# Pairwise bilinear interaction with a three-layer top network: first layer in two steps of two output tiles, its seventh input tile as two 64-row matmuls

## The reference, cut to what matters

```python
e = jnp.stack([tbl_f[ids[:, f]] for f in range(40)], axis=1)     # 2048 x 40 x 64
i_idx, j_idx = np.triu_indices(40, k=1)                          # 780 pairs
z = einsum('bpe,bpe->bp', einsum('bpd,pde->bpe', e[:, i_idx], W), e[:, j_idx])
h = jnp.concatenate([z, dense_ctx], axis=1)                      # 2048 x 796
h = jnp.maximum(h @ W_top1 + b_top1, 0.0)                        # 796 -> 512
h = jnp.maximum(h @ W_top2 + b_top2, 0.0)                        # 512 -> 256
y = h @ W_top3                                                   # 256 -> 1
```

## Time and profile before

| what | value |
|---|---|
| median of three runs | 1220.74 us |
| profiled execution: span on the core | 1221.2 us |
| PE busy | 1123.9 us (92%) |
| DVE busy | 957.6 us (78%) |
| ACT busy | 928.2 us (76%) |
| POOL busy | 633.7 us (52%) |
| mean share of the 16 DMA engines, by slice | 1 to 4 tenths |
| granted clock of PE, slices behind the first four | 0.9 or more of full speed |
| first layer L755: records, busy | 224 of mean 598 ns, 99.6 us |

### The profile page before, as it was taken

How to read it: one execution, slowest core, us unless ns; L and a number is a source line. 1 busy time by engine, 2 the same in 40 slices (tenths; PEclk the granted TensorE clock), 3 DMA queues, 4 the chain that set the end, 5 groups by cost and what they waited for, 6 DMA issues and landing times.

```text
span 1221.2 us, 45331 instructions
## 1 busy us (share of the span) xinstructions
PE 1123.9 (92%) x17376; PEld 401.1 (33%) x17376; DVE 957.6 (78%) x833; ACT 928.2 (76%) x6893; POOL 633.7 (52%) x742
## 2 busy tenths in 40 slices
PE   0468899999999999999999999999999999999999
PEld 0112333333333333333343333333333333333333
DVE  0258899999875688999967579999985768999970
ACT  0158878987676688999957588998967678998971
POOL 7877776555566555555556545544545554520000
PEclk9988999999999999999999999999999999999999
DMA  4122222222212222223222122222221212212100
GB/s 172 26 67 70 70 71 68 88 87 68 86 44 64 64 55 75 66 65 104 64 62 86 43 63 85 64 62 83 64 85 42 86 41 62 85 57 67 58 13 0
DMA packets 34199, 81.80 MB, mean 67 GB/s; under 512 B 12144, under 2 KB 12672, under 8 KB 33856
## 3 DMA queue, kind: packets, MB, share of 16 engines
q1 hardware_dynamic: 13472, 57.88, 14.3%
q0 software_dynamic: 20480, 21.01, 7.6%
q10 hardware_dynamic: 32, 0.01, 0.0%
HBM read 78.84 MB, written 0.01 MB: 65 GB/s over the span
## 4 chain that ended last, share of the span: by engine, by line
PE 53%; ACT 19%; DVE 11%; issue 11%; POOL 5%; DMA 0%; DVEq 0%; ACTq 0%
PE Ups L714 21%; ACT PB L555 17%; PE Zps L734 11%; PE Ups L707 9%; PE Ups L755 8%; DVE P L652 6%; DVE PB L641 3%; POOL VN L537 3%; DVE zB L625 2%; PE Ups L762 2%; PE Ups L693 2%; ACT P L574 1%; POOL stage L537 1%; ACT V L567 1%; POOL rest L534 1%
## 5 line engine op out<-in xcount | busy, mean ns | idle before, releaser
L555 ACT ACTIVATE PB<-PB 128x64 f32<-128x64 f32 x3344 | 801.1, 244 | 102.8 <-DVE PB L641 99.9
L652 DVE TENSOR_TENSOR P<-Ups,V 128x1024 f32<-128x1024 f32 x504 | 600.6, 1216 | 186.0 <-PE Ups L714 183.5
L537 POOL DMA_INDIRECT stage<-tbl,idx x512 | 483.2, 944 | 359.6 <-PE Ups L714 149.6
L555 ACT ACTIVATION_READ_ACCUMULATOR PB<-PB 128x1 f32 x3344 | 635.2, 190 | 0.0
L714 PE MATMUL Ups<-V,wf 64*32 64x512 f32 x8384 | 546.0, 600 | 32.4 <-ACT V L567 16.7
L641 DVE TENSOR_TENSOR PB<-Ups,VN 128x1024 f32<-128x1024 f32 x256 | 311.3, 1217 | 39.4 <-PE Ups L707 32.3
L707 PE MATMUL Ups<-wf,V 64*32 64x512 f32 x4096 | 279.2, 600 | 7.3 <-ACT V L567 2.8
L734 PE MATMUL Zps<-P,sel 64*32 64x512 f32 x4192 | 283.4, 591 | 0.0
L714 PEld LDWEIGHTS Ups<-V,wf 64*32 64x32 f32 x8384 | 149.5, 107 | 325.6 <-issue 168.0
L537 POOL DMA_INDIRECT VN<-tbl,idx x128 | 121.1, 946 | 93.1 <-PE Ups L714 39.0
L734 PEld LDWEIGHTS Zps<-P,sel 64*32 64x32 f32 x4192 | 81.6, 108 | 140.3 <-issue 134.2
(11 more groups left out here) (23 smaller groups left out, 110.1 us busy)
## 6 DMA issues: line engine op xcount, KB each, us to landing
wf<-w_units SPq DMA_DIRECT2D x84, 640.0 KB
stage<-tbl,idx POOLq DMA_INDIRECT x512
VN<-tbl,idx POOLq DMA_INDIRECT x128, 2.4
w1s<-w SPq DMA_DIRECT2D x1, 1792.0 KB, 11.0
w2s<-w SPq DMA_DIRECT2D x1, 512.0 KB, 11.9
idx<-ids SPq DMA_DIRECT2D x1, 320.0 KB, 3.0
z<-dense_t SPq DMA_DIRECT2D x4, 32.0 KB
y<-z ACTq DMA_DIRECT2D x4, 2.0 KB
```

The costliest lines, as they stand in the source:

```text
L537: pool.indirect_dma_start(out=natural_rows(m, t)[:, D * f:D * f + D], out_offset=None, in_=tables[field][:, :], in_offset=bass.IndirectOff ...
L555: last = act.activation(p, p, ACT.Copy, accum_out=zB[:, t, at:at + 1])
L652: dve.tensor_tensor(p, Ups[:, slot, :, :rows], v, ALU.mult).then_inc(mul_done, 1)
```

## The change

The first layer is done in two steps (`L1_STEPS`) of two output tiles each: a step fills both banks of its slot. It goes through tiles 1 to 6 of `z` with 128 x 128 weights for the first output tile and then for the second, and ends with two matmuls for tile 0, one for each bank, that use only 64 of the array's rows: the first reads rows 0 to 63 of tile 0, the second rows 64 to 127. For that, both halves of tile 0 hold all of its 32 rows. SP loads the dense inputs twice, and copies the strips of four rows from each half into the other by four small DMAs, all from its place ahead of one weight chunk. The weights of tile 0 are laid out by the host in the same doubled way. ACT does two activations behind each first-layer step. A group's top network has five steps instead of seven, 14 units apart instead of 10. The costs in `step_us` follow. The second and third layers are as before, under new numbers.

```diff
--- before.py
+++ after.py
@@ -176,7 +176,11 @@
 
 U_SLOTS, P_SLOTS, PB_SLOTS, STAGE_SLOTS = 3, 8, 3, 4
 LAG = 3
-MLP_STEPS = N1 // P128 + N2 // P128 + 1
+L1_STEPS, L2_STEPS = 2, N2 // P128
+MLP_STEPS = L1_STEPS + L2_STEPS + 1
+LAYER3 = MLP_STEPS - 1
+STRIP_ROWS = 2 * PART_ENDS[0]
+DENSE_LOADS = 2 * 3
 
 W_COLS, WB_COLS = 2 * D, 2 * JP * D
 CHUNK, W_SLOTS = 10 * W_COLS, 3
@@ -243,7 +247,7 @@
 
 
 RUN_PAIRS, TIES_US, RAMP_UNITS = 6, 62.0, 60
-MLP_APART = 10
+MLP_APART = 14
 
 
 def red_at(q):
@@ -301,7 +305,7 @@
 
 def step_us(step):
     if step[0] == "mlp":
-        return 6.15 if step[2] < 4 else 3.6 if step[2] < 6 else 0.7
+        return 11.1 if step[2] < L1_STEPS else 3.6 if step[2] < LAYER3 else 0.7
     return STEP_US[step[0]]
 
 
@@ -392,6 +396,11 @@
 Z0_BEFORE = {quad_units(_g * QUADS + PART_ENDS[0] - 1)[-1] + LAG + 1: _g for _g in range(GROUPS)}
 
 
+def outs_before(g, x):
+
+    return g * (4 + L2_STEPS + 1) + (2 * x if x < L1_STEPS else 4 + x - L1_STEPS)
+
+
 def z0_tile(g):
 
 
@@ -502,8 +511,14 @@
                 for g in range(GROUPS):
                     if c == w_of(J_LAST[g])[0] + 4:
                         sp.wait_ge(z0_done, g + 1)
-                        sp.dma_start(z[DENSE_ROW:DENSE_ROW + DENSE, z0_tile(g), :SIZES[g]],
-                                     dense_t[:, FIRST_ROW[g]:FIRST_ROW[g] + SIZES[g]]).then_inc(dense_loaded, 16)
+                        for half in range(2):
+                            at = D * half + DENSE_ROW
+                            sp.dma_start(z[at:at + DENSE, z0_tile(g), :SIZES[g]],
+                                         dense_t[:, FIRST_ROW[g]:FIRST_ROW[g] + SIZES[g]]).then_inc(dense_loaded, 16)
+                            for at in (0, 32):
+                                source, to = D * (1 - half) + at, D * half + at + STRIP_ROWS
+                                sp.dma_start(z[to:to + STRIP_ROWS, z0_tile(g), :],
+                                             z[source:source + STRIP_ROWS, z0_tile(g), :]).then_inc(dense_loaded, 16)
                 x = W_SETS[min(group, 1)] + load
                 sp.dma_start(wf[:, c % W_SLOTS, :], w_units[:, x * CHUNK:(x + 1) * CHUNK]
                              ).then_inc(wf_loaded[c % W_SLOTS], 16)
@@ -576,12 +591,12 @@
                 elif kind == "z0":
                     act.wait_ge(red_done, g * QUADS + PART_ENDS[0])
                     if g > 1:
-                        act.wait_ge(mlp_done, (g - 2) * MLP_STEPS + 4)
+                        act.wait_ge(mlp_done, (g - 2) * MLP_STEPS + L1_STEPS)
                     act.copy(z[:, z0_tile(g), :rows], Zps[:, 0, :rows]).then_inc(z0_copied, 1)
                 elif kind == "z":
                     act.wait_ge(red_done, g * QUADS + PART_ENDS[x])
                     if g:
-                        act.wait_ge(mlp_done, (g - 1) * MLP_STEPS + 4)
+                        act.wait_ge(mlp_done, (g - 1) * MLP_STEPS + L1_STEPS)
                     if g and 2 * x - 1 == H2:
                         act.wait_ge(y_written, 16 * g)
                     act.copy(z[:, 2 * x - 1:2 * x + 1, :rows], Zps[:, :, :rows]).then_inc(z_done, 1)
@@ -597,14 +612,17 @@
                     if g == 0 and x == 0:
                         act.wait_ge(consts_loaded, 16 * 5)
                     act.wait_ge(mlp_done, g * MLP_STEPS + x + 1)
-                    if x < 4:
-                        act.activation(h1[:, x, :rows], out, ACT.Relu, bias=b1s[:, x:x + 1]).then_inc(mlp_out, 1)
-                    elif x < 6:
-                        act.activation(z[:, H2 + x - 4, :rows], out, ACT.Relu, bias=b2s[:, x - 4:x - 3]
-                                       ).then_inc(mlp_out, 1)
+                    if x < L1_STEPS:
+                        for bank in range(2):
+                            n = 2 * x + bank
+                            act.activation(h1[:, n, :rows], Ups[:, slot, bank, :rows], ACT.Relu,
+                                           bias=b1s[:, n:n + 1]).then_inc(mlp_out, 1)
+                    elif x < LAYER3:
+                        n = x - L1_STEPS
+                        act.activation(z[:, H2 + n, :rows], out, ACT.Relu, bias=b2s[:, n:n + 1]).then_inc(mlp_out, 1)
                     else:
                         act.copy(z[:, H2, :P128], out[:, :P128]).then_inc(mlp_out, 1)
-                        act.wait_ge(mlp_out, (g + 1) * MLP_STEPS)
+                        act.wait_ge(mlp_out, outs_before(g + 1, 0))
                         act.dma_start(y[FIRST_ROW[g]:FIRST_ROW[g] + rows, :].rearrange("(t n) o -> t (n o)", n=P128),
                                       z[0:P128:32, H2, :P128]).then_inc(y_written, 16)
 
@@ -678,7 +696,7 @@
                 elif kind == "ztr":
                     pe.wait_ge(z_done, Z_COUNT[("zb", g, 0)])
                 else:
-                    pe.wait_ge(mlp_out, g * MLP_STEPS + x + 1)
+                    pe.wait_ge(mlp_out, outs_before(g, x + 1))
 
             for step in PE_STEPS:
                 kind, g, x = step
@@ -743,28 +761,35 @@
                             last = pe.transpose(Ups[:, slot, h, P128 * t:P128 * (t + 1)],
                                                 zB[:, t, P128 * h:P128 * (h + 1)], ident[:, :])
                     last.then_inc(ztr_done, 1)
-                elif x < 4:
+                elif x < L1_STEPS:
                     if x == 0:
                         pe.wait_ge(consts_loaded, 16 * 5)
-                        pe.wait_ge(dense_loaded, 16 * (g + 1))
-                    ready = [s for s in Z_STEPS if s[1] == g]
-                    tiles = [(None, z0_tile(g))] + [(s, k) for s in ready for k in z_tiles(s)]
-                    for n, (s, k) in enumerate(tiles):
-                        if x == 0 and s:
-                            pe.wait_ge(z_done, Z_COUNT[s])
-                        last = pe.matmul(Ups[:, slot, 0, :size], w1s[:, k % ZT, P128 * x:P128 * (x + 1)], z[:, k, :size],
-                                         start=n == 0, stop=n == ZT - 1)
+                    tiles = [(s, k) for s in Z_STEPS if s[1] == g for k in z_tiles(s)]
+                    for bank in range(2):
+                        n = 2 * x + bank
+                        for i, (s, k) in enumerate(tiles):
+                            if n == 0:
+                                pe.wait_ge(z_done, Z_COUNT[s])
+                            pe.matmul(Ups[:, slot, bank, :size], w1s[:, k, P128 * n:P128 * (n + 1)], z[:, k, :size],
+                                      start=i == 0, stop=False)
+                    if x == 0:
+                        pe.wait_ge(dense_loaded, 16 * DENSE_LOADS * (g + 1))
+                    for bank in range(2):
+                        n, half = 2 * x + bank, slice(D * bank, D * bank + D)
+                        last = pe.matmul(Ups[:, slot, bank, :size], w1s[half, 0, P128 * n:P128 * (n + 1)],
+                                         z[half, z0_tile(g), :size], start=False, stop=True)
                     last.then_inc(mlp_done, 1)
-                elif x < 6:
+                elif x < LAYER3:
+                    n = x - L1_STEPS
                     for k in range(4):
-                        if x == 4:
-                            pe.wait_ge(mlp_out, g * MLP_STEPS + k + 1)
-                        last = pe.matmul(Ups[:, slot, 0, :size], w2s[:, k, P128 * (x - 4):P128 * (x - 3)],
+                        if n == 0:
+                            pe.wait_ge(mlp_out, outs_before(g, 0) + k + 1)
+                        last = pe.matmul(Ups[:, slot, 0, :size], w2s[:, k, P128 * n:P128 * (n + 1)],
                                          h1[:, k, :size], start=k == 0, stop=k == 3)
                     last.then_inc(mlp_done, 1)
                 else:
                     for k in range(2):
-                        pe.wait_ge(mlp_out, g * MLP_STEPS + 5 + k)
+                        pe.wait_ge(mlp_out, outs_before(g, L1_STEPS + k + 1))
                         for t in range(TILES[g]):
                             last = pe.matmul(Ups[32 * t:32 * t + 1, slot, 0, :P128], w3s[:, k:k + 1],
                                              z[:, H2 + k, P128 * t:P128 * (t + 1)], start=k == 0, stop=k == 1)
@@ -796,14 +821,20 @@
     for n, item in enumerate(A_ITEMS):
         for block, half, i, j, _, _ in unit_pairs(item):
             row, tile = z_place(2 * n + block, half)
-            w1[row, tile] = W1[first[i] + j]
+            if tile:
+                w1[row, tile] = W1[first[i] + j]
+            else:
+                for to in range(2):
+                    away = row // D != to
+                    w1[D * to + row % D + STRIP_ROWS * away, tile] = W1[first[i] + j]
     for k in range(B_ROWS):
         for b in range(2):
             for j in range(2 * JP):
                 at = 4 * JP * (B_ROWS - 1 - k) + 2 * JP * b + j
                 w1[at % P128, ZB_TILE + at // P128] = W1[first[2 * k + b] + 2 * J0 + j]
     pairs = F * (F - 1) // 2
-    w1[DENSE_ROW:DENSE_ROW + DENSE, 0] = W1[pairs:]
```

(2 more changed lines are left out.)

## The result

The changed kernel takes 1230.72 us in the median (1227.71 to 1230.88), the kernel before 1220.74 us beside it: a ratio of 1.0076 with a 95% interval of 1.0061 to 1.0090, so it is slower, where 5.4 us less were forecast. The timed runs of the changed kernel are 1.8 us longer than their spans. Timed runs of the kernel before beside later experiments on equally fast chips have spans of 1217.5 to 1220.2 us, so its profiled execution, with 1221.2, was slower than all of them; the profiled one of after has 1229.0. That is why the two traces lie 7.8 us apart and the medians 10.0.

The account below looks back on a forecast made before the run. PE was taken to bound the kernel nearly everywhere; its own work -7.0, ACT behind steps +0.6 and the pauses' places +1.0 gave -5.4 us, so 1215.3 us in the median, with an 8-in-10 range of 1212.9 to 1219.8.

Parts of the forecast that it names:

- What bounds the kernel: Whole kernel: PE is the limit nearly everywhere behind the ramp, busy 1123.9 of 1221.2 us, DVE and ACT just behind.
- The first layer in the loop and the tail: PE's first-layer steps: 6.2 us gained in the loop's three groups and 0.8 in the tail, together -7.0 us.
- The change of block inside a step: PE, first-layer step: switching from 128 x 128 to 64 x 128 blocks costs 0.20 us, between 0.10 and 0.25.
- The way out: PE, end of a first-layer step in the loop: going to 64 x 32 blocks costs 0.05 us, between nothing and 0.10.
- The pair: PE, tile 0's two 64-row matmuls: halves run side by side and cost one matmul's 0.86 us; one behind the other, 1.72.
- the prediction's sign: What the trace should show for tile 0: 64-row records in pairs starting within 0.05 us, two pairs 0.43 us apart.
- SP: Six small DMAs instead of one hold a weight chunk up by 1.9 us; some 25 us cover it, so nothing is lost.
- ACT behind a step: Second activation delays ACT's next work by 0.59 us; loop steps cost nothing to 3.5 us, 0.6 taken.
- The place of the pauses: First-layer steps are pauses where ACT and DVE catch up; moving them costs nothing to 3.0 us, 1.0 taken.
- POOL: Five gathers go in a step of 11.1 us where three went in 6.15; counted nothing, give or take 1 us.
- slower: the long step starves the others: Rival: sums queued during long steps stall PE behind them, 1.7 us a step, 10 in all; about 1224.5 us, chance 0.08.
- ACT and DVE take most of it back: Rival: ACT and pause costs at their ends, 3.5 and 3.0 us, leave 0.5 us gain, 1220.2 us; chance 0.10.

Follow-up runs that it names:

- e3: Changed kernel without the sixteen small DMAs that copy strips of tile 0 between the halves; 1228.53 us, ratio 1.0069 to the kernel before.
- m1: Kernel before with its top-network steps 20 units apart instead of 10, on a slower chip; 1314.16 us, ratio 0.9941.
- f2: Kernel before with transposes and gathers where the planner puts them for the changed kernel, transposes kept behind steps; 1232.75 us, ratio 1.0080.
- g1: Changed kernel with one planner constant 1.6 instead of 1.9, so six gathers instead of five go ahead of a long step; 1224.85 us, ratio 1.0029.
- q2: Changed kernel with 12 of 16 sums of each of ACT's units left out; 1203.33 us, ratio 0.9855 to the kernel before.
- q1: Kernel before with 12 of 16 sums of each of ACT's units left out; 1208.12 us, ratio 0.9896.
- h0: Changed kernel whose planner sets no transpose within three units behind a unit of kind d, on a slower chip; 1310.43 us, ratio 1.0017.
- e, f, g and q: Follow-up runs with labels in these letters: planner orders, no small DMAs, gather room, ACT sums left out; kernel before beside them 1220.55, 1221.21 and 1220.31 us.
- h and k: Follow-up runs with no transposes behind units of kind d, or earlier copies into V, in either kernel; kernel before beside them 1308.03 us.
- m and n: Follow-up runs with steps 20 units apart or a planner set anew, or most of ACT's sums left out; kernel before beside them 1321.67 us.
- the first pair without sums: Kernel before and changed kernel, each with 12 of 16 sums of ACT's units left out, on a slower chip; 1301.50 and 1301.09 us.

## Why the prediction was wrong, point by point

- What bounds the kernel: right as far as it went. PE is the limit on average. That 38 us of waits are spread over the rest, set by how closely ACT and DVE follow, was read from the earlier trace rows only as two rates per unit.
- The first layer in the loop and the tail: right. 11.56 us a step against about 11.5, 23.11 against 23.3 us in the tail. The change of block inside a step was set down at 0.20 us; it is 0.09 ahead of the pair and 0.10 between its two passes. The way out was taken at 0.05 and is 0.10. The traces give 7.7 us less of PE's own work, against 7.0.
- The pair: both halves start within 7 ns of each other in either pass, so the halves overlap in full. The passes start 0.53 us apart, where the prediction's sign said 0.43; that is the 0.10 above. The pair's two passes take 0.96 us with that gap. The estimate made with the figure of the Trainium skill for four row tiles ("TensorE: Matmul & The Clock Gate", section "Measured speedup vs the span model"), 1.12 us for the pair, is not borne out for these two; the measurement decides.
- SP: right as far as is known. The wait for weights that would have shown it isn't there, and e3 puts the DMAs at 2.2 us by the medians, where nothing can't be excluded.
- ACT behind a step: the mechanism (a copy into `V` late in ACT's list) was the one that counted, but it was looked for only right behind the long steps, and set at 0.6 us. The waits at transposes grew by 10 us, and the largest stands at unit 507, some 90 units from the nearest long step.
- The place of the pauses: priced at 1.0 us from two averages. m1 shows that other places, with the order that the planner makes around them, move the time by 7.5 us.
- POOL, the step that failed: "I count nothing, give or take 1 us for an order that is shuffled". The new costs and places shift 48 of the 80 transposes by up to 15 units. That order, put into the kernel before, costs it 10 to 12 us (f2), and one more gather ahead of a long step gives the changed kernel 6 us back (g1). For all of ACT's copies, the pauses and the order the sum had 1.6 us; the traces show 15.5 us more of waits, two thirds of them at transposes.
- The rival "slower: the long step starves the others" had the right sign and the wrong place: it asked for 1.7 us behind each long step, and behind all six together there are 1.9, while q2 has the same steps and is faster than q1. The rival "ACT and DVE take most of it back" was the nearest; it was given a ceiling of 6.5 us by rows of a single order, and the loss under the new order is 15.5.

What stays open: how the 15.5 us of waits divide between copies that meet a pile of sums and pauses that come too early, since every repair of the order moved other transposes too. The order by itself accounts for 9.5 us of them in the kernel before; the other 6 appear only together with the new steps. A repair that changes one transpose and leaves all others wasn't tried.

## What to carry to other kernels

Where a planner makes the order of all engines from a few costs, a change of one step's cost or place is a change of everything behind it: compare the two orders before costing the edit, and give that shuffle its own line, sized by what another order of the old kernel does to the time (here 7.5 us one way and 10 to 12 the other, against a saving of 7). Here PE's saving reached the clock only with ACT's list short; so check who stands in front of a small copy that PE needs (here 26 sums and four copies, 8.7 us). Moving that one transpose behind the pile (h0) brought a wait of 4.2 us three units later, so a repair is checked along the whole list before it is believed.

## What the hardware showed that was not expected

The time depends on the chip. On the chips of the runs e, f, g and q the kernel before takes 1220 us, on those of h and k 1308 and of m and n 1322, and the granted clock is the same (0.98 to 1.00 of full speed in the timed runs of either). The sixteen records of a unit have no wait between them and normally start within 0.51 us. On the slower chips some of PE's units and reductions are torn: in h0 some 430 of about 1040 start their records over more than 0.56 us, 133 us in all above 0.50 us each, while in the kernel before on a faster chip 27 do, with 10 us. PE of h0:

```profile
159.87 2.87 PE L726 MATMUL Ups<-wf,V 64*32 64x512 f32 x15
162.18 0.61 PE L753 MATMUL Zps<-P,sel 64*32 64x512 f32 x1
162.58 0.59 PE L726 MATMUL Ups<-wf,V 64*32 64x512 f32 x1
162.63 3.02 PE L753 MATMUL Zps<-P,sel 64*32 64x512 f32 x14
```

The unit at 159.87 starts fifteen of its records and leaves the sixteenth for 162.58, 2.7 us behind the first. Nothing in the profile says what those records wait for, and whether the excess is the whole of the 87 us between the chips isn't shown. It is why times are compared only with the kernel before on the same chip, and why the first pair without sums decided nothing: 135 us of such excess in one, 139 in the other, with some 5 to be seen.
